# Reordering the first projection, two block seams and the last tiles of a one-core graph network kernel

## Chip, core and metric

The kernel runs on one core of a Trainium2 chip. The metric is the device time of one execution in microseconds (us), the median of several runs. Engines: TensorE (PE; PEld is its weight load), VectorE (DVE), ScalarE (ACT), GpSimd (POOL) and SyncE (SP, which issues the DMAs).

## What is computed

Four graph layers in a row on `x` (2048 × 256) and a 0/1 adjacency (2048 × 2048, mean density about 0.001), each with a residual and a layer norm:

```
x = _layernorm(x + _L0_gnn_ref(x, adj, L0_gnn_W_stack), axis=-1)
x = _layernorm(x + _L1_gnn_ref(x, adj, L1_gnn_W), axis=-1)
x = _layernorm(x + _L2_gnn_ref(x, adj, L2_gnn_W_neigh, L2_gnn_b_neigh, L2_gnn_W_self, L2_gnn_b_self), axis=-1)
x = _layernorm(x + _L3_gnn_ref(x, adj, L3_gnn_W1, L3_gnn_b1, L3_gnn_W2, L3_gnn_b2), axis=-1)
...
# L0, for each of two layers:  proj = x @ W; Wh, Ws = split(proj)
#   a = softmax(Wh @ Ws.T) * adj;  x = leaky_relu(a @ Wh + x)
# L1: relu(A_norm @ H @ W), A_norm = D^-1/2 (A + I) D^-1/2
# L2: relu((adj / deg) @ h @ W_neigh.T + b_neigh + h @ W_self.T + b_self)
# L3: h = relu(adj @ (x @ W1) + b1);  adj @ (h @ W2) + b2
```

## The kernel before

Products keep fp32 accuracy by splitting operands: ScalarE copies a value rounded (the high part, names ending in `_h`), VectorE subtracts it from the original (the low part, `_l`), and TensorE runs high × high, high × low and low × high (`exact3`). Each engine has its own instruction list, written by hand and run in order; semaphores join them. A waiting instruction holds up everything behind it on its engine. `NT` = 16 row tiles of 128 rows, `NCH` = 4 chunks of 512 columns (4 tiles each, `TPC`), `KT` = 2 halves of the 256 features.

**The start.** TensorE runs 8 fill products (`keep_busy`), transposes the first 512 rows of `x` (`features(0)`, one bank for each half of the features), runs 3 more fill products, and then projects queries and keys chunk by chunk. For the first chunk `project_part` makes the two query halves one after the other, six products each into a bank of `scores`, and all of it waits for the low part of the query weights (`s_wgl`). ScalarE makes the high parts of the transposed features, GpSimd the high part of the query weights, VectorE the low parts.

**The blocks.** After two attention layers come the blocks: block 1 (L1), block 2 (L2), block 3a and 3b (the two products with the adjacency of L3). In the code they are `C`, `Dg`, `E` and `F`, and `aggs[k]`. The transposed adjacency lies in `adjr` as the stationary operand; the moving operand is `pm` (512 columns: high and low half), for block 3a `pme` (256 columns). `sum_over(k, t, first, stop)` adds the products of row tile `t` over input tiles `first` to `stop` into one of 4 banks (`sums`: `ob`, a part of `scores`, `tb0`, `tb1`), so tile `t + 4` needs the bank that VectorE's `total` of tile `t` has read. `chunk(k, c, tiles)` is 4 products for each tile named. Tiles 0 to 3 are summed first, as far as their moving operand is ready; `body` sums tiles 4 to 15, 48 chunks, and puts between them the steps of tiles 0 to 13:

- a *turn* (`C_rows`, `D_rows`): TensorE transposes a finished, normalized tile, as soon as VectorE has written its rows (`xs` in block 1, `keep` in block 2);
- a *projection* (`C_project`, `D_project`): the products with the next block's weights, as soon as ScalarE and VectorE have made `xt_h` and `xt_l` of the turned tile.

Tiles 14 and 15 are turned and projected at the *seam*, among the first sums of the next block. VectorE's list for a tile is `total`, `rows_lo` of the tile before, `residual` (add, statistics, variance), `norm` (after ScalarE's root: inverse, normalized rows), `self_term` and `moving_lo`. At the first seam `split(q)` also makes the low part of block 2's moving operand, in five pieces of 4, 4, 4, 2 and 2 tiles, behind ScalarE's high part.

**The end.** `across_sums` sums block 3b for groups of tiles, `sums_hi` and `sums_lo` split a group's sums (at the tiles in `LEAD` = 0, 4, 8, 11, 13), `F_project` makes the last product of each tile, and VectorE adds the residual (`with_residual`), then `statistics`, `mean_variance`, `inverse`, `normed`. SyncE stores each tile.

Of the kernel before, what the change touches and what calls it, by code (L numbers as in the profile page):

```python
# [13 lines left out]
P = 128  # L14
# [29 lines left out]
def ge(eng, signal, count):  # L44

    if isinstance(count, int) and count <= 0:
        return
    if isinstance(signal, Signal):
        eng.wait_ge(signal.sem, count + signal.base)
    else:  # L50
        eng.wait_ge(signal, count)
# [8 lines left out]
def adjacency_resnet(nc, x, adj, w_gat, w_gcn, w_neigh, b_neigh, w_self, b_self, w1, b1, w2, b2, out):  # L60
    N, D = x.shape
    NT = N // P
    KT = D // P
    CH = 512
# [23 lines left out]
    with ctx:  # L88
# [1127 lines left out]
        def _(dve):  # L1216
# [599 lines left out]
            def exact():  # L1816

                for k, a in enumerate(aggs):
                    _, rows_lo, total, residual, norm, self_term, steps = parts(k, a, True)
                    with_residual, statistics, mean_variance, inverse, normed, moving_lo = steps  # L1820
                    split = parts(k + 1, aggs[k + 1], True)[0] if not a.last else None

                    def slot(b, u, ep=True, fin=True):
                        p, pp = before(b, u), before(b, u, 2)
                        if ep:
                            total(*p)
                        if fin:
                            rows_lo(*pp)
                        if ep:
                            residual(*p)  # L1830
                            norm(*p)
                        if fin:
                            self_term(*pp)
                            moving_lo(*pp)

                    if a is F:
                        for t in range(NT + 1):
                            y, z = (t // 2 * 2, t % 2), ((t - 1) // 2 * 2, (t - 1) % 2)
                            if t in LEAD:
                                sums_lo(LEAD.index(t))  # L1840
                            if t < NT:
                                with_residual(*y)
                            if t:
                                inverse(*z)
                            if t < NT:
                                statistics(*y)
                            if t:
                                normed(*z)
                            if t < NT:
                                mean_variance(*y)  # L1850
                        continue
                    if a is E:
                        for t in range(NT):
                            total(t // 2 * 2, t % 2)
                            if t:
                                hidden_lo(t - 1)
                        hidden_lo(NT - 1)
                        continue
                    slot(0, 1, fin=False)
                    slot(2, 0)  # L1860
                    slot(2, 1)
                    unrolled(slot)
                    slot(NT - 2, 0)
                    if not a.last:
                        total(NT - 2, 0)
                        rows_lo(NT - 4, 1)
                        residual(NT - 2, 0)
                        if a is C:
                            split(0)
                        norm(NT - 2, 0)  # L1870
                        self_term(NT - 4, 1)
                        moving_lo(NT - 4, 1)
                        if a is C:
                            split(1)
                        total(NT - 2, 1)
                        rows_lo(NT - 2, 0)
                        residual(NT - 2, 1)
                        norm(NT - 2, 1)
                        if a is C:
                            split(2)  # L1880
                        self_term(NT - 2, 0)
                        moving_lo(NT - 2, 0)
                        if a is C:
                            split(3)
                        rows_lo(NT - 2, 1)
                        self_term(NT - 2, 1)
                        moving_lo(NT - 2, 1)
                        if a is C:
                            split(4)
# [9 lines left out]
        def _(pe):  # L1899
            def mm(o, l, r, start, stop):  # L1900
                return nc.tensor.matmul(o, l, r, start=start, stop=stop)  # L1901
# [34 lines left out]
            def keep_busy(n):  # L1936

                for _ in range(n):
                    mm(xb0[:, 0:P], ident[:, :], ident[:, :], True, True)

            keep_busy(8)
            features(0)
            keep_busy(3)

            def n_rows(t, u):
                pe.wait_ge(n_new, t + 1)
# [12 lines left out]
            def layer(l, g, previous):  # L1959
# [3 lines left out]
                pe.sem_inc(g.wsl.sem, 1)  # L1963
                pe.sem_inc(g.staged.sem, 1)
                pe.sem_inc(g.vl.sem, 1)
                pe.wait_ge(s_wgl[l], 1)
                if l:
                    ge(pe, G[l - 1].ex, 4 * NT)

                def rows_turned(i):  # L1970
# [6 lines left out]
                def project_part(i, o, bank):  # L1977

                    gs, os = bass.ts(i, CH), slice(o * P, (o + 1) * P)
                    if not l and isinstance(i, int) and i + o == 0:  # L1980

                        for k in range(KT):
                            pe.wait_ge(s_x0l, k + 1)
                            mm(bank[:, :], wg_h[:, k, os], xtall_h[:, k, gs], k == 0, False)
                            mm(bank[:, :], wg_h[:, k, os], xtall_l[:, k, gs], False, False)
                            last = mm(bank[:, :], wg_l[:, k, os], xtall_h[:, k, gs], False, k == KT - 1)
                        last.then_inc(g.prod.sem, 1)
                        return
                    exact3(bank[:, :], [(wg_h[:, k, os], wg_l[:, k, os], xtall_h[:, k, gs], xtall_l[:, k, gs])
                                        for k in range(KT)]).then_inc(g.prod.sem, 1)  # L1990

                def project(i):

                    if l or i:
                        rows_turned(i)
                    for o in range(2 * KT):
                        if not l and o == KT:
                            features(i + 1)
                            if i == 0:
                                pe.wait_ge(s_wgl[0], 2)  # L2000
                        if o < KT:
                            ge(pe, g.staged, KT * i + 1)
                        else:
                            ge(pe, g.wsl, KT * i + 1)
                        if l and o == 2 * KT - 1:
                            ge(pe, G[l - 1].z, NT)
                        project_part(i, o, scores[:, o * CH:(o + 1) * CH])
# [298 lines left out]
            def exact():  # L2306
# [45 lines left out]
                def chunk(k, c, *tiles):  # L2352
                    for t in tiles:
                        sum_over(k, t, c * TPC, (c + 1) * TPC)
# [67 lines left out]
                def body(k, rows, project):  # L2422

                    ended = iter([(step, i) for i in range(NT) for step in (rows, project)])

                    def steps(n):
                        for _ in range(n):
                            step, i = next(ended)
                            step(*tile(i))

                    parts, total = NCH * (NT - BANKS), 2 * (NT - 2)
                    for t in range(BANKS, NT):
                        for c in range(NCH):
                            chunk(k, c, t)
                            if project:
                                n = NCH * (t - BANKS) + c
                                steps((n + 1) * total // parts - n * total // parts)

                chunk(0, 0, 0, 1, 2, 3)
# [5 lines left out]
                end_sums(0, NT - NCH)  # L2445
                body(0, C_rows, C_project)

                C_rows(NT - 2, 0)
                chunk(1, 0, 0, 1)
                C_project(NT - 2, 0)  # L2450
                chunk(1, 0, 2, 3)
                chunk(1, 1, 0, 1)
                C_rows(NT - 2, 1)
                chunk(1, 1, 2, 3)
# [2 lines left out]
                end_sums(1, NT - NCH)  # L2457
                body(1, D_rows, D_project)

                D_rows(NT - 2, 0)  # L2460
                chunk(2, 0, 0, 1)
                D_project(NT - 2, 0)
                chunk(2, 0, 2, 3)
                chunk(2, 1, 0, 1, 2, 3)
                chunk(2, 2, 0, 1)
                D_rows(NT - 2, 1)
                chunk(2, 2, 2, 3)
                for t in range(BANKS):
                    sum_over(2, t, NT - 4, NT - 2)
                D_project(NT - 2, 1)  # L2470
                for t in range(BANKS):
                    sum_over(2, t, NT - 2, NT - 1)
                end_sums(2, NT - 1)
                body(2, None, None)

                across_sums(0, 0, NT)
# [40 lines left out]
```

## Time and profile before

| | |
|---|---|
| three runs | 735.72, 736.05 (median), 737.24 us |
| profiled execution | 736.77 us; span from first to last instruction 735.0 us |
| TensorE busy | 719.0 us (98%), 3984 products |
| VectorE, ScalarE, GpSimd busy | 481.4, 337.3, 324.6 us |
| mean granted TensorE clock | 0.997 |

A busy share is a mean over stages. Matmuls are pipelined, so one of 512 columns is shown with about 0.4 us though the next starts 0.23 us after it: spacing is read from start to start. In a row of the timeline the bracket at the end is the idle time of that engine before the row, and what ended it.

### The profile page before, as it was taken

The page shows a single profiled execution, that of the slowest core. Times are in us where ns is not written, and L with a number is a line of the kernel's source. Part 1 is how long each engine was busy: PE and PEld are TensorE (multiplying, and loading weights), DVE is VectorE, ACT ScalarE, POOL GpSimd, SP SyncE. Part 2 cuts the span into 40 slices and gives each one's busy share as a digit, 9 for nine tenths or more (in the row PEclk, how much of TensorE's full clock was granted, in tenths as well). Part 3 has the DMA queues.
Part 4 walks back from the last instruction along what each step waited for, and adds up shares of the span by engine and source line. Part 5 has one row for each costly group of instructions (what it writes and reads, how often), then busy time and mean ns, then how long its engine had stood idle before and what let it go on. Part 6 is the DMA issues. An engine that isn't in the chain of part 4 may idle for free.

```text
span 735.0 us, 13241 instructions
## 1 busy us (share of the span) xinstructions
PE 719.0 (98%) x3984; PEld 613.1 (83%) x3984; DVE 481.4 (66%) x1111; ACT 337.3 (46%) x785; POOL 324.6 (44%) x346
## 2 busy tenths in 40 slices
PE   8999999999999999999999999999999999989995
PEld 7888888888888888888888888888777687779985
DVE  3767777777776664655755755754677848875366
ACT  4666565665656455365465465451222412221121
POOL 1157676676766316454454454384664000003200
PEclk9999999999999999999999999999999999999998
DMA  7042424324242201732231232246862222210012
GB/s 271 29 144 93 166 87 144 113 101 156 86 153 76 111 18 58 166 119 74 87 128 71 86 128 72 86 103 126 194 171 87 72 64 66 66 44 2 1 44 74
DMA packets 63139, 72.39 MB, mean 98 GB/s; under 512 B 36336, under 2 KB 56432, under 8 KB 58992
## 3 DMA queue, kind: packets, MB, share of 16 engines
q1 hardware_dynamic: 63088, 71.78, 31.3%
q8 instruction: 24, 0.39, 0.2%
q14 instruction: 27, 0.22, 0.1%
HBM read 46.60 MB, written 16.78 MB: 86 GB/s over the span
## 4 chain that ended last, share of the span: by engine, by line
PE 93%; DVE 3%; issue 1%; ACT 1%; POOL 1%; DMA 0%; SPq 0%; DVEq 0%; POOLq 0%; ACTq 0%
PE scores L1901 39%; PE ob L1901 29%; PE tb L1901 11%; PE tb L2070 7%; PE xb L1901 3%; PE tb L2014 1%; DMA self_term_scratch<-rst 0%; PE tb L1920 0%; PE xb L2095 0%; PE xb L1949 0%; POOL adjr L648 0%; SPq L477 0%; DVE xt_l L1222 0%; PE scores L2371 0%; DVE zb L1611 0%
## 5 line engine op out<-in xcount | busy, mean ns | idle before, releaser
L671 POOL TENSOR_TENSOR prob<-prob,arow 128x512 f32<-128x512 f32 x128 | 191.9, 1521 | 145.9 <-ACT prob L875 145.8
L1901 PE MATMUL ob<-val,stationary 128*128 128x512 f32 x960 | 186.7, 344 | 0.0
L1901 PEld LDWEIGHTS ob<-val,stationary 128*128 128x128 f32 x960 | 146.7, 189 | 18.4
L1222 DVE TENSOR_TENSOR stationary<-tb,stationary 128x512 fp32r<-128x512 f32 x128 | 85.4, 687 | 57.3 <-ACT stationary L776 56.1
L1901 PE MATMUL scores<-wst_h,whs_h 128*128 128x512 f32 x256 | 102.6, 401 | 0.0
L1901 PE MATMUL scores<-wst_h,whs_l 128*128 128x512 f32 x256 | 100.0, 390 | 0.0
L1901 PE MATMUL scores<-wst_l,whs_h 128*128 128x512 f32 x256 | 99.8, 390 | 0.0
L1319 DVE TENSOR_REDUCE row_values<-scores 128x1 f32<-128x512 f32 x128 | 85.9, 683 | 13.5 <-PE scores L1901 12.0
L776 ACT ACTIVATE stationary<-tb 128x512 fp32r<-128x512 f32 x128 | 72.9, 595 | 42.4 <-PE tb L2070 40.9
L875 ACT ACTIVATE prob<-scores,row_values 128x512 f32<-128x512 f32 x128 | 86.8, 690 | 11.4 <-DVE row_values L1326 11.4
L2070 PE MATMUL tb<-ident,prob 128*128 128x128 f32 x512 | 71.7, 272 | 0.0
L1901 PE MATMUL tb<-pm,adjr 128*128 128x512 f32 x256 | 66.7, 399 | 0.0
L2070 PEld LDWEIGHTS tb<-ident,prob 128*128 128x128 f32 x512 | 60.0, 140 | 5.7
L733 POOL TENSOR_TENSOR keep<-keep,bout 128x256 f32 x16 | 11.7, 743 | 106.7 <-PE tb L1901 101.1
L1061 ACT ACTIVATE sd<-mv,constants 128x1 f32<-128x1 f32 x48 | 14.1, 295 | 93.6 <-DVE mv L1691 93.6
L1901 PEld LDWEIGHTS scores<-wst_h,whs_l 128*128 128x128 f32 x256 | 48.1, 188 | 10.3
L1901 PEld LDWEIGHTS scores<-wst_h,whs_h 128*128 128x128 f32 x256 | 48.1, 188 | 9.3
L1901 PEld LDWEIGHTS scores<-wst_l,whs_h 128*128 128x128 f32 x256 | 48.3, 189 | 7.9
L1901 PEld LDWEIGHTS tb<-pm,adjr 128*128 128x128 f32 x256 | 46.3, 188 | 9.0
L1359 DVE SCALAR_TENSOR_TENSOR arow<-arow 128x2048 bf16<-128x2048 f32 x16 | 43.6, 2725 | 3.0 <-issue 3.0
L776 ACT ACTIVATE xt_h<-xb 128x256 fp32r<-128x256 f32 x30 | 11.5, 384 | 62.4 <-PE xb L1949 43.7
L648 POOL CAST adjr<-at 128x512 fp32r<-128x512 bf16 x64 | 40.0, 668 | 0.0
(227 smaller groups left out, 1191.7 us busy)
## 6 DMA issues: line engine op xcount, KB each, us to landing
arow<-in_adj SPq DMA_DIRECT2D x32, 1024.0 KB, 5.2
adjacency_halves<-arow SPq DMA_DIRECT2D x16, 512.0 KB, 3.0
features_scratch<-xs SPq DMA_DIRECT2D x32, 128.0 KB, 1.9
xres<-features_scratch SPq DMA_DIRECT2D x32, 128.0 KB, 2.1
keep<-in_x SPq DMA_DIRECT2D x4, 512.0 KB, 7.2
xres<-in_x SPq DMA_DIRECT2D x16, 128.0 KB, 2.0
self_term_scratch<-rst SPq DMA_DIRECT2D x16, 128.0 KB, 1.7
rin<-self_term_scratch SPq DMA_DIRECT2D x16, 128.0 KB, 2.2
```

The lines of the kernel that those rows point to most:

```text
L648: nc.gpsimd.tensor_copy(adjr[:, t, js.start * P:js.stop * P], at16[r][:, js, :].rearrange("p a i -> p (a i)")).then_inc(s_conv, 1)
L671: nc.gpsimd.tensor_tensor(prob[u][:, cs], prob[u][:, cs], arow[u][:, cs], ALU.mult).then_inc(g.msk.sem, 1)
L733: nc.gpsimd.tensor_tensor(keep[:, t, :], keep[:, t, :], bout[:, :], ALU.add).then_inc(s_kb, 1)
L776: return nc.scalar.activation(dst, src, ACT.Copy, **kw)
L875: nc.scalar.activation(prob[u][:, cs], scores[:, cs], ACT.Exp, bias=nmax[u][:, :], accum_out=rs[u][:, c:c + 1]).then_inc(g.ex.sem, 1)
L1061: nc.scalar.activation(sd[:, u:u + 1], mv[:, u, 1:2], ACT.Sqrt, bias=eps[:, :])\
L1222: return nc.vector.tensor_tensor(dst, v, h.bitcast(F32), ALU.subtract)
L1319: nc.vector.reduce_max(mx[u][:, c:c + 1], scores[:, c * CH:(c + 1) * CH], AX.X)\
L1359: nc.vector.scalar_tensor_tensor(arow16[:, :], arow[u][:, :], 1.0, arow16[:, :], ALU.mult, ALU.not_equal, accum_out=bits[:, bass.ds(t, 1)])\
L1901: return nc.tensor.matmul(o, l, r, start=start, stop=stop)
L2014: last = nc.tensor.transpose(bank[:, at:at + P], wht_g[:, k, (2 * h + a) * P:(2 * h + a + 1) * P], ident[:, :])
L2070: last = nc.tensor.transpose(tb[c % 2][:, q * P:(q + 1) * P], prob[u][:, j * P:(j + 1) * P], ident[:, :])
```

## The change

At the start the three fill products are taken out, and the first chunk's query halves are made side by side by `first_queries`: the high × high products as soon as their operands are there, then the others, each pair with a wait of its own. In `body` the steps are spread over 47 chunks and not 48, so the last projection stands ahead of the last chunk. At both seams sums of the next block stand ahead of the turn of tile 14, and VectorE's order at the first seam follows: the first piece of `split` ahead of tile 14's `residual`, the second behind tile 15's `total`. In block 3b `sums_lo` of the groups at tiles 11 and 13 stands behind that tile's add and statistics, and the last tiles' steps are interleaved.

```diff
                     if a is F:
-                        for t in range(NT + 1):
+                        for t in range(NT - 2):
                             y, z = (t // 2 * 2, t % 2), ((t - 1) // 2 * 2, (t - 1) % 2)
-                            if t in LEAD:
+                            if t in LEAD and t <= TPC * 2:
                                 sums_lo(LEAD.index(t))
...
                             if t:
                                 inverse(*z)
-                            if t < NT:
-                                statistics(*y)
+                            statistics(*y)
+                            if t in LEAD and t > TPC * 2:
+                                sums_lo(LEAD.index(t))
                             if t:
                                 normed(*z)
...
+                        inverse(NT - 4, 1)
+                        normed(NT - 4, 1)
+                        with_residual(NT - 2, 0)
+                        statistics(NT - 2, 0)
+                        with_residual(NT - 2, 1)
+                        mean_variance(NT - 2, 0)
+                        statistics(NT - 2, 1)
+                        inverse(NT - 2, 0)
+                        mean_variance(NT - 2, 1)
+                        normed(NT - 2, 0)
+                        inverse(NT - 2, 1)
+                        normed(NT - 2, 1)
...
                         total(NT - 2, 0)
                         rows_lo(NT - 4, 1)
-                        residual(NT - 2, 0)
                         if a is C:
                             split(0)
+                        residual(NT - 2, 0)
                         norm(NT - 2, 0)
                         self_term(NT - 4, 1)
                         moving_lo(NT - 4, 1)
+                        total(NT - 2, 1)
+                        rows_lo(NT - 2, 0)
                         if a is C:
                             split(1)
-                        total(NT - 2, 1)
-                        rows_lo(NT - 2, 0)
                         residual(NT - 2, 1)
...
             features(0)
-            keep_busy(3)
...
+                def first_queries():
+
+                    def both(w, x, k, start=False):
+                        return [mm(scores[:, o * CH:(o + 1) * CH], w[:, k, o * P:(o + 1) * P], x[:, k, 0:CH],
+                                   start, False) for o in range(KT)]
+
+                    pe.wait_ge(s_wqh, 1)
+                    for k in range(KT):
+                        pe.wait_ge(s_x0h, k + 1)
+                        both(wg_h, xtall_h, k, k == 0)
+                    pe.wait_ge(s_x0l, 1)
+                    both(wg_h, xtall_l, 0)
+                    pe.wait_ge(s_wgl[0], 1)
+                    for k in range(KT):
+                        both(wg_l, xtall_h, k)
+                    pe.wait_ge(s_x0l, KT)
+                    for o in range(KT):
+                        mm(scores[:, o * CH:(o + 1) * CH], wg_h[:, 1, o * P:(o + 1) * P], xtall_l[:, 1, 0:CH],
+                           False, True).then_inc(g.prod.sem, 1)
...
-                    parts, total = NCH * (NT - BANKS), 2 * (NT - 2)
+                    parts, total = NCH * (NT - BANKS) - 1, 2 * (NT - 2)
...
-                            if project:
-                                n = NCH * (t - BANKS) + c
+                            n = NCH * (t - BANKS) + c
+                            if project and n < parts:
                                 steps((n + 1) * total // parts - n * total // parts)
...
+                chunk(1, 0, 0, 1)
                 C_rows(NT - 2, 0)
-                chunk(1, 0, 0, 1)
+                chunk(1, 0, 2, 3)
                 C_project(NT - 2, 0)
-                chunk(1, 0, 2, 3)
                 chunk(1, 1, 0, 1)
...
+                chunk(2, 0, 0, 1)
+                chunk(2, 1, 0, 1)
                 D_rows(NT - 2, 0)
-                chunk(2, 0, 0, 1)
+                chunk(2, 2, 0, 1)
+                chunk(2, 0, 2)
                 D_project(NT - 2, 0)
-                chunk(2, 0, 2, 3)
-                chunk(2, 1, 0, 1, 2, 3)
-                chunk(2, 2, 0, 1)
+                chunk(2, 0, 3)
+                chunk(2, 1, 2, 3)
                 D_rows(NT - 2, 1)
                 chunk(2, 2, 2, 3)
-                for t in range(BANKS):
+                for t in range(2):
                     sum_over(2, t, NT - 4, NT - 2)
                 D_project(NT - 2, 1)
-                for t in range(BANKS):
-                    sum_over(2, t, NT - 2, NT - 1)
-                end_sums(2, NT - 1)
+                for t in range(2, BANKS):
+                    sum_over(2, t, NT - 4, NT - 1)
+                for t in range(2):
+                    sum_over(2, t, NT - 2, NT)
+                for t in range(2, BANKS):
+                    sum_over(2, t, NT - 1, NT)
```

TensorE's list at the first seam, before, from the last chunk of block 1 to the first sums of block 2 (`scores<-w2h,xt_h` begins a projection of six products, `xb<-ident,xs` is the turn of tile 14):

```order
L1901 MATMUL tb<-pm,adjr 128x512 x4
L1901 MATMUL scores<-w2h,xt_h 128x512 [waits agg_self_term_ready,agg_projection_kept,agg_rows_lo]
...
L2236 MATMUL xb<-ident,xs 128x128 [waits agg_rows_lo,agg_rows_ready]
...
L1901 MATMUL ob<-pm,adjr 128x512 [waits agg_moving_lo_block2,agg_sum_ready]
...
L1901 MATMUL scores<-pm,adjr 128x512 [waits agg_moving_lo_block2,agg_sum_ready]
```

The same place after:

```order
L1912 MATMUL scores<-w2h,xt_h 128x512 [waits agg_self_term_ready,agg_projection_kept,agg_rows_lo]
...
L1912 MATMUL tb<-pm,adjr 128x512 x4
L1912 MATMUL ob<-pm,adjr 128x512 [waits agg_moving_lo_block2,agg_sum_ready]
...
L1912 MATMUL scores<-pm,adjr 128x512 [waits agg_moving_lo_block2,agg_sum_ready]
...
L2261 MATMUL xb<-ident,xs 128x128 [waits agg_rows_lo,agg_rows_ready]
```

The projection of tile 13 went ahead of the last chunk, and the first two chunks of block 2 went ahead of the turn of tile 14.

TensorE's list at the second seam, before, from the last chunk of block 2 to the projection of tile 14 (`pme` products are block 3a's, `xb<-ident,keep` is the turn of tile 14):

```order
1523 L1901 MATMUL tb<-pm,adjr 128x512 x4
1524 L1901 MATMUL scores<-w3a,xt_h 128x256
...
1528 L2371 MATMUL xb<-ident,keep 128x128 x2
1529 L1901 MATMUL ob<-pme,adjr 128x256 x4
1530 L1901 MATMUL scores<-pme,adjr 128x256 x4
1531 L1901 MATMUL scores<-w3a,xt_h 128x256
```

The same place after:

```order
1520 L1912 MATMUL tb<-pm,adjr 128x512 x4
1521 L1912 MATMUL ob<-pme,adjr 128x256 x4
1522 L1912 MATMUL scores<-pme,adjr 128x256 x4
1523 L1912 MATMUL ob<-pme,adjr 128x256 x4
1524 L1912 MATMUL scores<-pme,adjr 128x256 x4
1525 L2396 MATMUL xb<-ident,keep 128x128 x2
1526 L1912 MATMUL ob<-pme,adjr 128x256 x4
1527 L1912 MATMUL scores<-pme,adjr 128x256 x4
1528 L1912 MATMUL tb<-pme,adjr 128x256 x4
1529 L1912 MATMUL scores<-w3a,xt_h 128x256
```

Sixteen products of block 3a now stand ahead of the turn of tile 14, and twelve between the turn and the projection where there were eight.

VectorE's list at the end, before, tiles 14 and 15 behind the normalization of tile 12 (the add reads `scores` and `keep`, `xs` and `xres` take the normalized rows):

```order
1259 L1691 BN_AGGR mv<-norm_values 128x2
1260 L1661 TENSOR_TENSOR zb<-scores,keep 128x256
1261 L1701 RECIPROCAL rstd<-sd 128x1
1262 L1684 BN_STATS norm_values<-zb 128x6
1263 L1720 TENSOR_SCALAR xres<-zb,mv,rstd 128x256
1264 L1691 BN_AGGR mv<-norm_values 128x2
1265 L1701 RECIPROCAL rstd<-sd 128x1
1266 L1720 TENSOR_SCALAR xres<-zb,mv,rstd 128x256
```

The same place after:

```order
1255 L1701 RECIPROCAL rstd<-sd 128x1
1256 L1720 TENSOR_SCALAR xs<-zb,mv,rstd 128x256
1257 L1661 TENSOR_TENSOR zb<-scores,keep 128x256
1258 L1684 BN_STATS norm_values<-zb 128x6
1259 L1661 TENSOR_TENSOR zb<-scores,keep 128x256
1260 L1691 BN_AGGR mv<-norm_values 128x2
1261 L1684 BN_STATS norm_values<-zb 128x6
1262 L1701 RECIPROCAL rstd<-sd 128x1
1263 L1691 BN_AGGR mv<-norm_values 128x2
1264 L1720 TENSOR_SCALAR xres<-zb,mv,rstd 128x256
1265 L1701 RECIPROCAL rstd<-sd 128x1
1266 L1720 TENSOR_SCALAR xres<-zb,mv,rstd 128x256
```

Tile 13 is now finished before tile 14 begins, and the adds and statistics of tiles 14 and 15 stand ahead of the inverses of both.

## Rows read from the trace of the kernel before

**Rows 1.** The page: its head, busy time of the engines, and the chain that ended last.

```profile
span 735.0 us, 13241 instructions
...
PE 719.0 (98%) x3984; PEld 613.1 (83%) x3984; DVE 481.4 (66%) x1111; ACT 337.3 (46%) x785; POOL 324.6 (44%) x346
...
PE 93%; DVE 3%; issue 1%; ACT 1%; POOL 1%; DMA 0%; SPq 0%; DVEq 0%; POOLq 0%; ACTq 0%
```

**Rows 2.** Timeline of the start: start, length, engine, line, operation, count, idle before.

```profile
5.12 1.91 PE L1920 MATMUL tb<-ident,keep 128*128 128x128 f32 x8
...
6.82 0.96 PE L1901 MATMUL xb<-ident 128*128 128x128 f32 x6
...
7.07 0.60 ACT L776 ACTIVATE xtall_h<-tb 128x512 fp32r<-128x512 f32 x1 [0.26 <-PE tb L1920]
...
8.19 0.49 PE L1901 MATMUL scores<-xtall_h,wg_h 128*128 128x512 f32 x1 [0.41 <-DVE wg_l L1222]
```

**Rows 3.** Chain that ended last, at the start: start, length, engine, output, count.

```profile
8.19 3.06 PE scores L1901 x12
11.25 0.88 PE tb L1920 x8
12.12 2.77 PE scores L1901 x12
```

**Rows 4.** Timeline of TensorE, block 1's last tiles and the first seam.

```profile
567.07 0.38 PE L2236 MATMUL scores<-ident,xs 128*128 128x128 f32 x2
...
580.87 0.44 PE L2236 MATMUL xb<-ident,xs 128*128 128x128 f32 x2 [1.13 <-DVE xs L1727]
...
583.58 0.51 PE L1901 MATMUL scores<-w2h,xt_h 128*128 128x512 f32 x1 [0.41 <-DVE xt_l L1222]
```

**Rows 5.** Timeline of VectorE, block 1's last tiles and the first seam.

```profile
565.86 0.41 DVE L1727 TENSOR_SCALAR xs<-zb,mv,rstd 128x256 f32<-128x256 f32 x1
...
579.10 1.19 DVE L1222 TENSOR_TENSOR pm<-keep,pm 128x1024 fp32r<-128x1024 f32 x1
...
580.41 0.41 DVE L1727 TENSOR_SCALAR xs<-zb,mv,rstd 128x256 f32<-128x256 f32 x1
```

**Rows 6.** Timeline of TensorE, the second seam.

```profile
656.68 0.44 PE L2371 MATMUL xb<-ident,keep 128*128 128x128 f32 x2 [1.46 <-DVE keep L1709]
...
658.45 0.39 PE L1901 MATMUL scores<-w3a,xt_h 128*128 128x256 f32 x1 [0.38 <-DVE xt_l L1222]
...
662.84 0.38 PE L2371 MATMUL scores<-ident,keep 128*128 128x128 f32 x2
...
664.96 0.28 PE L1901 MATMUL scores<-w3a,xt_h 128*128 128x256 f32 x1
...
667.73 2.19 PE L1901 MATMUL ob<-pme,adjr 128*128 128x256 f32 x16 [0.36 <-DVE zb L1608]
```

**Rows 7.** Timeline of VectorE in block 2, normalized rows of tiles 4, 14 and 15.

```profile
616.51 0.41 DVE L1709 TENSOR_SCALAR keep<-zb,mv,rstd 128x256 f32<-128x256 f32 x1
...
656.21 0.41 DVE L1709 TENSOR_SCALAR keep<-zb,mv,rstd 128x256 f32<-128x256 f32 x1
...
660.12 0.41 DVE L1709 TENSOR_SCALAR keep<-zb,mv,rstd 128x256 f32<-128x256 f32 x1
```

**Rows 8.** Timeline of VectorE in block 3b, its first tile and its last.

```profile
701.08 0.43 DVE L1684 BATCH_NORM_STATS2 norm_values<-zb 128x6 f32<-128x256 f32 x1
701.66 0.18 DVE L1691 BATCH_NORM_AGGREGATE mv<-norm_values 128x2 f32<-128x6 f32 x1 [0.16 <-DVE norm_values L1684]
...
726.30 0.42 DVE L1222 TENSOR_TENSOR fsum_l<-xb,fsum_h 128x256 fp32r<-128x256 f32 x1 [0.79 <-ACT fsum_h L776]
726.64 0.41 DVE L1661 TENSOR_TENSOR zb<-scores,keep 128x256 f32<-128x256 f32 x1
...
730.95 0.16 DVE L1701 RECIPROCAL rstd<-sd 128x1 f32<-128x1 f32 x1 [0.36 <-ACT sd L1061]
731.14 0.41 DVE L1720 TENSOR_SCALAR xres<-zb,mv,rstd 128x256 f32<-128x256 f32 x1
```

More of the change, by code:

```diff
@@ L1836, in exact @@
                     if a is F:
-                        for t in range(NT + 1):
+                        for t in range(NT - 2):
                             y, z = (t // 2 * 2, t % 2), ((t - 1) // 2 * 2, (t - 1) % 2)
-                            if t in LEAD:
+                            if t in LEAD and t <= TPC * 2:
                                 sums_lo(LEAD.index(t))
-                            if t < NT:
-                                with_residual(*y)
+                            with_residual(*y)
                             if t:
                                 inverse(*z)
-                            if t < NT:
-                                statistics(*y)
+                            statistics(*y)
+                            if t in LEAD and t > TPC * 2:
+                                sums_lo(LEAD.index(t))
                             if t:
                                 normed(*z)
-                            if t < NT:
-                                mean_variance(*y)
+                            mean_variance(*y)
+                        inverse(NT - 4, 1)
[10 more added lines that the diff above has]
+                        normed(NT - 2, 1)
                         continue
@@ L1965, in layer @@
                 pe.sem_inc(g.vl.sem, 1)
-                pe.wait_ge(s_wgl[l], 1)
                 if l:
+                    pe.wait_ge(s_wgl[l], 1)
                     ge(pe, G[l - 1].ex, 4 * NT)
@@ L1979, in project_part @@
                     gs, os = bass.ts(i, CH), slice(o * P, (o + 1) * P)
[L1980 to L1988, printed above, removed]
                     exact3(bank[:, :], [(wg_h[:, k, os], wg_l[:, k, os], xtall_h[:, k, gs], xtall_l[:, k, gs])
                                         for k in range(KT)]).then_inc(g.prod.sem, 1)
+                def first_queries():
[15 more added lines that the diff above has]
+                           False, True).then_inc(g.prod.sem, 1)
                 def project(i):
@@ L1995, in project @@
                         rows_turned(i)
+                    else:
+                        first_queries()
                     for o in range(2 * KT):
+                        if not l and isinstance(i, int) and i == 0 and o < KT:
+                            continue
                         if not l and o == KT:
```

## The prediction

> **What bounds the kernel.** I read the page first, then TensorE's waits, then the rows around each place that the diff touches. The page gives TensorE 719.0 of 735.0 us [rows 1]: at most 16.0 us of the span are without a matmul, so an edit can win only by closing a named hole, or by shortening the stretch after the last matmul. In the chain that ended last 93% is TensorE [rows 1]; between the start and the first seam its matmuls follow each other at 0.23 us for 512 columns (twelve in 2.77 us [rows 3]). What is won at the start is therefore handed on: nothing later waits for a clock time, only for TensorE's own products.
>
> The holes that the diff touches are these. At the start the first product waits until 8.19 us for VectorE's low part of the query weights, 0.41 us of it idle [rows 2]; three fill products stand before it. At the first seam TensorE waits 1.13 us for the new rows of tile 14, and 0.41 us for their low part [rows 4]. At the second seam the same two waits are 1.46 and 0.38 us, and one of 0.36 us ends the seam [rows 6]. Behind the last matmul VectorE finishes three tiles one after the other, and the last has to wait 0.36 us for its root [rows 8].
>
> **The start.** Before, twelve products run from 8.19 to 11.25 us: 12 × 0.23 and 0.29 for starting up [rows 3]. After, the first two need only the first copy of the high features and the high query weights, and run where the fill stood (6.82 [rows 2]). The next two need the second high copy, which ends at 7.07 + 0.60 = 7.67 [rows 2]. I allow 0.06 for the release: ten products from 7.73 on end at 7.73 + 2.30 + 0.29 = 10.32. The low weights come before the seventh product (7.73 + 0.29 + 4 × 0.23 = 8.94, against 8.19), so that wait is covered. Gain 11.25 − 10.32 = 0.93 us. The query banks are now released together, not one after the other, but ScalarE copies the next features first and comes to them later anyway. Bounds: 0.5 (a second start-up and a late copy) and 0.95. I take 0.9.
>
> The three fill products are taken out, so what do they do for TensorE's clock? The granted clock reads full in the page, but the rows show two speeds: the first eight transposes take 1.91 us [rows 2], eight equal ones at 11.25 take 0.88 [rows 3], as 1.2 against 2.4 GHz would give. The six fill records take 0.96 us together, the quicker pace already [rows 2]. So the rise came before or while the first of them ran, after eight plain products and the transposes, and they cannot have caused it. By the Trainium skill ("TensorE: Matmul & The Clock Gate", Part 4: PE-mode transpose) transposes do not count as activity for the clock; by that rule removing plain products just here would be the wrong edit, and the time that of rival (c) below, 735.1. This trace leaves it open, since eight plain products stood ahead of the transposes, but the fill was not needed here.
>
> **The first seam (block 1 to block 2).** Before, TensorE is ready for the turn of tile 14 at 580.87 − 1.13 = 579.74, and VectorE ends the rows at 580.41 + 0.41 = 580.82 [rows 4, 5]. After, eight sum products (8 × 0.23 = 1.85) stand ahead of that turn, so TensorE comes at 581.6, some 0.8 after the rows. VectorE's low half of block 2's first moving piece (1.19 us [rows 5]) is put ahead of tile 14's residual; it was already inside that chain, between variance and root, where 0.36 of it lay beside ScalarE. So it costs the rows between 0 and 0.4 us, inside the 0.8. The 0.41 us: before the low part of tile 14 stood behind the second such piece and tile 15's total; now the piece stands behind it, and eight products lie between turn and projection as before. The sums moved up need the first piece (long ready by then) and, for the fourth bank, tile 15's total, which is now ahead of the second piece. So both waits go: 1.54 us, and two restarts at 0.1 to 0.29 [rows 3].
>
> Against it: the bodies now spread 28 turns and projections over 47 chunks, not 48, so in the second half most turns come one chunk (4 × 0.23 = 0.92) sooner. In block 1 tile 11's rows end at 565.86 + 0.41 = 566.27 and its turn is at 567.07 [rows 5, 4]: 0.80 spare, 0.12 too little. Such a shortage is paid once, since a late TensorE is late for the next turn too; I put 0.3 to 0.5 us for the whole body. Net 1.54 + 0.3 − 0.4 = 1.4 us; bounds 0.8 and 1.9.
>
> **The second seam (block 2 to block 3).** Here VectorE sets the pace: from 616.51 to 656.21 it ends ten tiles, 3.97 us each [rows 7], while TensorE's share of a tile is 48 × 0.92 / 14 = 3.2 and some 0.5 for a turn and a projection, 3.7. A turn one chunk sooner only waits there, at no cost to VectorE. Before, TensorE is ready for turn 14 at 656.68 − 1.46 = 655.22. After, sixteen products of 256 columns (2.19 with a restart [rows 6], so 0.12 apart) stand ahead of it: 657.2, or 658.0 if TensorE first lost 0.9 in the body. The rows are there at 656.21 + 0.41 = 656.62 [rows 7]: no wait. The price is that tile 14's turn, and with it VectorE's next step, comes 0.5 to 1.3 later, so tile 15's rows slip from 660.53 to about 661.3. They had room: TensorE turned them only at 662.84, 2.31 after they were done [rows 6, 7]. After, 24 half-width products and a projection lie between the turns (24 × 0.12 + 0.5 = 3.4), so turn 15 is at 661.4. From there to the last projection there were sixteen products (662.84 to 664.96, 2.12), now twelve (1.6), hence 663.0; the path through the low part to the first tile of block 3 (664.96 to 667.73, 2.77) is unchanged. 665.8 against 667.73: 1.9. I take 1.8; bounds 0.9 and 2.2. All is counted from the start of block 2, which the first seam moves.
>
> **The end.** VectorE's steps start 0.31 to 0.34 apart where none waits [rows 8]. Before, from the last low half (726.30) to the end of the last normalization (731.14 + 0.41) are 5.25 us. After, tile 13's add and statistics stand ahead of that low half, in time in which VectorE waited for ScalarE. Behind it come, start to start: low half 0.34, normalization of 12 0.31, variance of 13 to its inverse 0.54 (0.18 and the 0.36 wait), inverse 0.19, normalization 0.31, add of 14 0.43, statistics 0.34, add of 15 0.34, variance of 14 0.21, statistics of 15 to variance 0.58 (701.08 to 701.66), variance to inverse 0.54, inverse 0.19, normalization 0.41: 4.73. Gain 0.5 us; bounds 0.2 (the last two stores now lie about half a microsecond apart) and 0.6. The other low half, at tile 11, is some 0.4 us later; TensorE's product that needs it has about 0.1 to spare.
>
> **Sum.** 0.9 + 1.4 + 1.8 + 0.5 = 4.6 us. The profiled execution took 736.77 (span 735.0 and 1.77 around it), 0.72 above the median of the runs shown, 736.05. So 732.2 for that execution, 730.4 in span, and 731.5 for the median.
>
> **Rivals.** (a) *The waits only move on.* At both seams half of the gain is taken by the next in-order step of VectorE (the second piece behind tile 14's low part; tile 15's rows at the second seam): 0.9 + 0.7 + 0.9 + 0.4 = 2.9, 733.1. For it: every cover is a margin of under 1 us. (b) *The seams give nothing*, since VectorE's chain and not TensorE's order sets the end of each block: 0.9 + 0.5 = 1.4, 734.7. Against it: at the second seam tile 15's rows lie 2.31 us idle. (c) *The clock stays low at the start* without the fill: twelve products and eight transposes at double time cost 2.77 + 0.88 = 3.65; the seams remain: 736.05 − 4.6 + 3.65 = 735.1, no difference. (d) *Slower: the turns come too soon.* If VectorE is the pace in block 1 as in block 2, TensorE waits up to a chunk at each of the six turns shifted, 5.6 us there, and with the same again in block 2 11.1, against the 4.6 gained: 742.6. It decides from 6.1 us of new waits in the bodies on. Against it: the 0.80 spare at tile 11, and that such waits do not add up.
>
> **How the numbers follow.** Forecast 0.66 (730.2 to 732.6), (a) 0.17, (b) 0.08, (c) 0.05, (d) 0.04. The range 730.2 to 733.9 takes in the forecast and (a) with its bounds. Faster by over 0.2% (1.47 us, about what a measurement of this kernel tells from no change) means below 734.6: forecast and (a), and a little of (b): 0.85. Same: most of (b), and (c): 0.11. Slower: (d): 0.04.
>
> **What would show it.** In the changed profile: the first product at about 6.9 and the first values' transposes 0.9 us sooner; no wait of TensorE for tile 14's rows or low part at either seam; in block 2 waits for rows spread over the body; half a microsecond less between TensorE's last product and the last normalization. The forecast is wrong if transposes at 10 us still take 0.2 us each, if a new wait of about a microsecond stands in a seam, or if block 1's body shows more than half a microsecond of new waits.

## The result, and the profile after

The changed kernel takes 731.08 us (median of four runs, 730.37 to 732.37); the kernel before, beside it, 736.64. The ratio is 0.9926 with a 95% interval of 0.9904 to 0.9948: 3.8 to 7.1 us less, about 5.5. A second group of runs on another chip gave 730.88 against 735.74, 0.9938 (0.9921 to 0.9955). The forecast was 731.5 us, 4.6 less. The profiled execution took 732.37 us with a span of 730.6.

The page of the changed kernel, as [rows 1]: its head, busy times, and the chain that ended last.

```profile
span 730.6 us, 13229 instructions
PE 718.5 (98%) x3978; PEld 611.8 (84%) x3978; DVE 482.6 (66%) x1111; ACT 337.1 (46%) x785; POOL 324.7 (44%) x346
PE 93%; DVE 2%; ACT 1%; issue 1%; SPq 1%; DMA 1%; POOL 1%; DVEq 0%; POOLq 0%; ACTq 0%
```

TensorE's busy time hardly moved; its holes did: the span without a matmul is 12.1 us, before 16.0. The timeline of TensorE at the start, as [rows 2, 3]:

```profile
5.12 1.92 PE L1931 MATMUL tb<-ident,keep 128*128 128x128 f32 x8
6.96 1.49 PE L1912 MATMUL scores<-xtall_h,wg_h 128*128 128x512 f32 x4
9.65 0.62 PE L1912 MATMUL scores<-xtall_l,wg_h 128*128 128x512 f32 x2
10.11 1.03 PE L1931 MATMUL tb<-ident,keep 128*128 128x128 f32 x8
```

The first product is at 6.96, and the first values' transposes at 10.11, where the timeline of before has them at 11.08. They are at the quick pace without the fill. The first seam, TensorE and then VectorE, as [rows 4, 5]:

```profile
580.88 0.38 PE L2261 MATMUL xb<-ident,xs 128*128 128x128 f32 x2
582.96 0.39 PE L1912 MATMUL scores<-w2h,xt_h 128*128 128x512 f32 x1
586.20 0.38 PE L2261 MATMUL scores<-ident,xs 128*128 128x128 f32 x2
```
```profile
579.42 0.41 DVE L1727 TENSOR_SCALAR xs<-zb,mv,rstd 128x256 f32<-128x256 f32 x1
581.72 0.42 DVE L1222 TENSOR_TENSOR xt_l<-xb,xt_h 128x256 fp32r<-128x256 f32 x1 [0.64 <-ACT xt_h L776]
```

Neither row of TensorE for tile 14 (580.88 turn, 582.96 projection) has a bracket: both waits of [rows 4] are gone. The rows of tile 14 end at 579.83, 1.05 ahead of the turn, their low part at 582.14, 0.82 ahead of the projection. The second seam, as [rows 6]:

```profile
655.12 0.38 PE L2396 MATMUL xb<-ident,keep 128*128 128x128 f32 x2
656.77 0.28 PE L1912 MATMUL scores<-w3a,xt_h 128*128 128x256 f32 x1
658.66 0.38 PE L2396 MATMUL scores<-ident,keep 128*128 128x128 f32 x2
663.07 2.18 PE L1912 MATMUL ob<-pme,adjr 128*128 128x256 f32 x16 [0.24 <-DVE zb L1608]
```

Turn 14 (655.12) and its projection (656.77) wait for nothing; the wait that ends the seam is 0.24 us, before 0.36. VectorE's last low half and last normalization, as [rows 8]:

```profile
721.60 0.43 DVE L1222 TENSOR_TENSOR fsum_l<-xb,fsum_h 128x256 fp32r<-128x256 f32 x1
722.80 0.16 DVE L1701 RECIPROCAL rstd<-sd 128x1 f32<-128x1 f32 x1 [0.36 <-ACT sd L1061]
725.91 0.41 DVE L1720 TENSOR_SCALAR xres<-zb,mv,rstd 128x256 f32<-128x256 f32 x1
```

From the one to the other are 4.31 us, before 4.84. But the span ends 4.69 us after 725.91, and before 3.86 after 731.14. What the end won came back behind it, in this profile.

### The profile page after: what moved, and what is told of

Same layout as the page of the kernel before. It is cut to its first block, busy times and chain, and to the rows that moved or that the text cites. A ratio compares the mean times of both kernels' runs of the same rounds, so it can differ in the third digit from the quotient of the medians.

```text
span 730.6 us, 13229 instructions
## 1 busy us (share of the span) xinstructions
PE 718.5 (98%) x3978; PEld 611.8 (84%) x3978; DVE 482.6 (66%) x1111; ACT 337.1 (46%) x785; POOL 324.7 (44%) x346
## 4 chain that ended last, share of the span: by engine, by line
PE 93%; DVE 2%; ACT 1%; issue 1%; SPq 1%; DMA 1%; POOL 1%; DVEq 0%; POOLq 0%; ACTq 0%
PE scores L1912 39%; PE ob L1912 29%; PE tb L1912 11%; PE tb L2095 7%; PE xb L1912 3%; PE tb L2039 1%; SPq L477 1%; PE tb L1931 1%; DMA self_term_scratch<-rst 0%; PE xb L2120 0%; PE xb L1959 0%; POOL adjr L648 0%; DMA xres<-features_scratch 0%; PE scores L2396 0%; PE xb L2396 0%
```

## The experiments

All twelve kernels were profiled and timed, in three groups of four on one chip each. The first four each do one part of the change on the kernel before, with that part of the diff shown above; the bodies stay spread over 48 chunks in them.

**The start alone.** The edit: `first_queries`, no three fill products.

> The kernel before with the new start alone (first queries side by side, high products first, no three fill products). My theory: 0.9 to 1.0 us less, so 735.1 where the kernel before takes 736.05; the first values' transposes at about 10.1 us and still some 0.9 us for eight. Rival, the clock stays low without the fill: those transposes take 1.9 us and the time is no lower or up to 2.7 us higher. Rival, the lead is lost again at the seams, where VectorE's chain sets the pace: no change, and longer waits in the seams by as much.

Measured: 0.9986 (0.9976 to 0.9996), 1.0 us less; first values' transposes at 10.12. At both seams the waits stand as long as before (1.13 and 0.41 us, 1.47 and 0.38), 0.8 to 0.9 us sooner: nearly the whole lead is handed on.

**The first seam alone.** The edit: TensorE's order at the seam, VectorE's order of the two pieces.

> The kernel before with the first seam alone (eight sum products ahead of tile 14's turn, VectorE's two pieces moved), bodies spread over 48 chunks as before. My theory: both waits of TensorE for tile 14 at that seam (1.13 and 0.41 us) and two restarts go, 1.5 to 1.9 us less. Rival, the waits only move on: 0.7 us less and a new wait of TensorE at that seam. Rival, VectorE's chain sets the block's end: no change, the wait stands at tile 15 or in block 2's body.

Measured: 0.9973 (0.9963 to 0.9983), 2.0 us less. The turns of tiles 13 and 15 are 10.11 us apart (576.38 to 586.49), before 11.97 (576.77 to 588.74): 1.86, the two waits and the restarts, with no new wait.

**The second seam alone.** The edit: TensorE's order at that seam.

> The kernel before with the second seam alone, bodies spread over 48 chunks as before. My theory: the waits of 1.46 and 0.38 us at that seam go, the one that ends it stays, 1.8 to 2.1 us less. Rival, the waits only move on (tile 15's rows come late): 0.9 us less, TensorE waiting about 1 us at tile 15's turn. Rival, VectorE's chain sets the end: no change.

Measured: 0.9962 (0.9948 to 0.9976), 2.8 us less, more than expected. Turns 14 and 15 and the last wait of the seam:

```profile
657.31 0.38 PE L2371 MATMUL xb<-ident,keep 128*128 128x128 f32 x2
660.87 0.44 PE L2371 MATMUL scores<-ident,keep 128*128 128x128 f32 x2
665.34 0.85 PE L1901 MATMUL ob<-pme,adjr 128*128 128x256 f32 x5 [0.23 <-DVE zb L1608]
```

From block 2's first turn (601.57) to 665.34 are 63.77 us, before 66.41 (601.32 to 667.73): 2.64. It is more than the two waits of 1.46 and 0.38 us and the restarts behind them, since the two waits in front of the last products shrink as well, from 0.58 and 0.36 us (at 666.63 and 667.73 before) to 0.22 and 0.23 (at 664.25 and 665.34). What the time shows beyond 2.64, 0.2 us, lies far inside its interval (1.8 to 3.8 us less).

**The end alone.** The edit: VectorE's last tiles interleaved.

> The kernel before with VectorE's last tiles interleaved and nothing else. My theory: the last normalization ends 0.5 us sooner after TensorE's last product, and the time falls by 0.5 us. Rival, the stores take it back: in the profile of the changed kernel the last store is issued 0.64 us after the one ahead of it, not 1.05, and lands after 3.7 us, not 2.9; by this the last normalization ends 0.5 us sooner and the time does not change or rises by up to 0.3 us.

Measured: 0.9996 (0.9987 to 1.0005), no change that can be told; the interval goes from 1.0 us less to 0.4 more, so it does not rule out the expected 0.5 by itself. The rows speak for the rival. The last normalization is 4.33 us behind the last low half, but the span ends 3.99 us after it. The last stores of its profile:

```profile
L593 SPq DMA_DIRECT2D out_rows<-xres x2: 332/332/333, 731.8 to 732.4; - x2
DMA to landing us min/median/max: 3.0/3.2/3.3
```

They are issued 0.6 us apart and land 3.3 and 3.0 us after their issue; two of the same profile, at 725.1 and 726.5, took 1.7 each.

**The fill put back, and no fill at all.** Both are edits of the changed kernel:

```diff
 keep_busy(8)
 features(0)
+keep_busy(3)
```
```diff
-keep_busy(8)
 features(0)
```

> The changed kernel with the three fill products put back behind the first transposes. My theory: they are not needed for the clock; the first two products, which could run at 6.96 us, come behind 0.96 us of fill (six records), the next two wait for the second high copy anyway (7.72), so the start loses 0.3 to 0.5 us and no more. Rival, the fill holds the clock up: the first four products get quicker and the time falls by 0.2 us or more.

> The changed kernel without the eight plain products ahead of the first transposes, so that TensorE has done nothing but transposes before its first products. My theory, transposes raise the clock as products do: the transposes of 10 us take some 0.9 us for eight and the time is within 0.5 us of the changed kernel's. Rival, the rule that transposes do not count: the twelve first products take twice as long (0.23 us more each, 2.8 us in all) and the transposes behind them 1.9 us; the time rises by 1.5 to 3.7 us.

Measured with the fill back: 0.9937 (0.9923 to 0.9951), the changed kernel's own ratio, and no gain. The loss of 0.3 to 0.5 us that I expected is too small for this interval; in its profile there is none. The first product stands at 6.81 behind the fill, and at 6.82 without it in the profile of the second run of the changed kernel, whose clock also rose early (rows in the last section): there TensorE waits 0.34 us for ScalarE's copy, and the fill lies largely in that time. No profile has the fill with a clock that rises late, as in the changed kernel's first profile. Without any: 0.9950 (0.9935 to 0.9964), 1.0 us slower than the kernel with the fill beside it, and by the ratios 0.9 to 1.8 slower than the changed kernel in its two groups. TensorE's start there:

```profile
4.62 1.94 PE L1931 MATMUL tb<-ident,keep 128*128 128x128 f32 x8 [4.62 <-DMA keep<-in_x]
6.51 2.07 PE L1912 MATMUL scores<-xtall_h,wg_h 128*128 128x512 f32 x4
8.38 1.05 PE L1912 MATMUL scores<-xtall_l,wg_h 128*128 128x512 f32 x2
9.23 1.21 PE L1912 MATMUL scores<-xtall_h,wg_l 128*128 128x512 f32 x4
10.73 1.03 PE L1931 MATMUL tb<-ident,keep 128*128 128x128 f32 x8
```

The first six products start 0.42 to 0.47 us apart, half speed, the last six 0.23 to 0.26; the values' transposes are at 10.73. My limit of half a microsecond was too small, and the rival, all twelve at half speed and the transposes too, is wrong as well.

**VectorE's order at the first seam as before.** The edit, in the changed kernel (each `if` joined with its body on one line):

```diff
 rows_lo(NT - 4, 1)
-if a is C: split(0)
 residual(NT - 2, 0)
+if a is C: split(0)
 ...
+if a is C: split(1)
 total(NT - 2, 1)
 rows_lo(NT - 2, 0)
-if a is C: split(1)
```

> The changed kernel with VectorE's own order at the first seam as before (first piece between tile 14's variance and root, second piece and tile 15's total ahead of tile 14's low part). My theory, from the changed kernel's rows: the low part then ends near 582.5 us, still ahead of tile 14's projection at 582.96, so no change, at most 0.2 us. Rival, VectorE's order is what took the 0.41 us wait away: 0.4 to 0.8 us more, with TensorE waiting for that low part.

Measured: 0.9933 (0.9919 to 0.9947), no difference. TensorE's turn of tile 14 is at 579.84, its projection at 581.91, neither with a wait; VectorE's rows and low part are there in time:

```profile
577.88 0.41 DVE L1727 TENSOR_SCALAR xs<-zb,mv,rstd 128x256 f32<-128x256 f32 x1
578.54 1.22 DVE L1222 TENSOR_TENSOR pm<-keep,pm 128x1024 fp32r<-128x1024 f32 x1
580.67 0.42 DVE L1222 TENSOR_TENSOR xt_l<-xb,xt_h 128x256 fp32r<-128x256 f32 x1
```

The second piece fills the time in which VectorE waits for ScalarE's half (0.64 us at that place in the changed kernel). With the old order the rows of tile 14 even end 1.55 us ahead of the turn (578.29 and 579.84), with the new one 1.05: a piece moved ahead of them only used up cover. At this seam TensorE's order did all of the work, with the bodies over 47 chunks; over 48, where the cover of the rows is 0.14 us in the next experiment's profile (579.79 and 579.93), VectorE's old order was not run.

**The bodies spread over 48 chunks.** The edit, in the changed kernel:

```diff
-parts, total = NCH * (NT - BANKS) - 1, 2 * (NT - 2)
+parts, total = NCH * (NT - BANKS), 2 * (NT - 2)
```

> The changed kernel with the bodies' turns and projections spread over 48 chunks again, so that those of the second half come one chunk (0.92 us) later. My theory: in block 1 no wait is there to be saved, so 0 to 0.3 us less there; in block 2 the last projection comes closer to the seam, whose rows for tile 14 then are late by up to 0.5 us. Net within 0.5 us of the changed kernel. Rival, the earlier turns cost the bodies 0.4 us or more: faster by that much.

Measured: 0.9914 (0.9900 to 0.9929), 730.12 us; the two kernels beside it, whose edits of the changed one had no measured effect, took 731.55 (fill) and 730.96 (VectorE's order), 0.8 to 1.4 more. The intervals overlap, but the rows bear it out, and with them the rival. From block 2's first turn to the last wait of its seam:

```profile
597.94 0.38 PE L2396 MATMUL xb<-ident,keep 128*128 128x128 f32 x2
661.69 0.50 PE L1912 MATMUL ob<-pme,adjr 128*128 128x256 f32 x2 [0.23 <-DVE zb L1608]
```

63.75 us, and 64.30 in the changed kernel (598.77 to 663.07). No wait of TensorE's for tile 14's rows came, as I had thought it might. Where the 0.55 us go can be read from the starts of TensorE's products between block 2's first turn and its turn 14. Mostly they start 0.23 us apart, at some places up to 0.32; at nine turns and projections it is 0.38 to 0.45 in each of the six profiles with 47 chunks, at six in each of the eight with 48. Three more pauses of some 0.17 us make 0.5.

**The changed kernel once more, and with the old end.** The second takes back the interleaved end.

> The changed kernel once more, beside the three others of this group on one chip. My theory, from the rows of the runs so far: 4.5 to 5.5 us less than the kernel before. It is the measure for the other three and for the fill and body experiments, whose differences from the changed kernel are under 1 us.

> The changed kernel with VectorE's order of the last block as before. My theory: the last normalization ends 5.25 us after the start of the last low half, not 4.72, so it ends 0.5 us later; the time rises by 0.2 to 0.5 us. Rival, the stores take back what the interleaving wins, since the last two are issued closer together: the time does not change.

Measured: 0.9938 and 0.9930 (0.9915 to 0.9946): 730.88 and 730.73 us, no difference, the rival again: the old end, which I expected to be 0.2 to 0.5 us slower, is 0.15 quicker in the median. With the old end the last normalization is 4.85 us behind the low half, but the span ends 3.62 us after it.

**A version with both bodies at 48, and the end further interleaved.** The edit of the end:

```diff
+with_residual(NT - 2, 0)
 inverse(NT - 4, 1)
 normed(NT - 4, 1)
-with_residual(NT - 2, 0)
```

> The changed kernel with the bodies spread over 48 chunks and, at the end, tile 14's add ahead of tile 13's inverse, where VectorE waits 0.36 us for a root. My theory: from the first turn of block 2 to the last wait of its seam 63.75 us, not 64.30 (so in the run with 48 alone), and 0.4 us less in block 1; at the end 0.3 us less from the last low half to the last normalization: 0.8 to 1.3 us less than the changed kernel. Rival, the end's part is lost behind the last normalization, in the stores: 0.5 to 0.9 us less, and the last store lands later after its issue.

Measured: 0.9924 (0.9908 to 0.9940), 730.20 us, 0.7 under the changed kernel beside it, with intervals that overlap. Block 2 takes 63.76 us as at 48; the last normalization is 3.95 us behind the low half, and the span ends 4.85 after it. So by these rows the gain is the bodies', and the end's is lost in the stores. No version here was better than the spread over 48.

**The wait of the second seam filled.** The kernel before, with plain products in that wait (the loop on one line):

```diff
 body(1, D_rows, D_project)
+ge(pe, Dg.xtl, NT - 3)
+for _ in range(8): mm(xb[0][:, 0:P], ident[:, :], ident[:, :], True, True)
 D_rows(NT - 2, 0)
```

> The kernel before with eight plain products (sixteen records, about 1.1 us) put into TensorE's wait for tile 14's rows at the second seam. The wait itself stays. Theory, the wait lets TensorE's clock fall in some executions: the granted clock is 1.00 in the microseconds behind that seam in the profile, no execution has a mean clock of 0.994 or less, and the median falls by 0 to 0.3 us. Rival, the falls come from elsewhere: one execution in six still shows them.

Measured: 1.0001 (0.9990 to 1.0012); no time is won. The products take 1.84 us (654.51 to 656.35), not the 1.1 that I reckoned, so they take the whole wait, and turn 14 comes 0.2 us later after block 2's first turn than before (55.59 and 55.36). None of its twelve executions has a mean granted clock under 0.996. What the clock has to do with it can be seen in a profile in which the wait is not filled: the kernel with the end alone, at the second seam, which its edit does not touch (windows of 4 us: TensorE's busy time, granted clock, DMA):

```profile
654.00:658.00 4.00, 2.48 (x16) 1.00 0.00 0
658.00:662.00 4.00, 3.66 (x18) 0.57 0.02 4
662.00:666.00 4.00, 4.00 (x36) 1.00 0.00 0
```
```profile
656.57 0.44 PE L2382 MATMUL xb<-ident,keep 128*128 128x128 f32 x2 [1.46 <-DVE keep L1709]
659.25 2.02 PE L1912 MATMUL tb<-pme,adjr 128*128 128x256 f32 x8
664.26 0.38 PE L2382 MATMUL scores<-ident,keep 128*128 128x128 f32 x2
```

The same eight products of 256 columns in the profile of the filled kernel:

```profile
658.42 1.17 PE L1901 MATMUL tb<-pme,adjr 128*128 128x256 f32 x8
```

Behind the waits of 1.46 and 0.38 us the clock falls to its lower level (0.51 from 658.3 to 661, so 1.2 of 2.4 GHz), the eight products take 2.02 us and not 1.17, and turn 15 comes 7.69 us after turn 14, not 6.16 as in [rows 6]. That costs 1.5 us.

## Why the forecast was right, and where its terms were off

The intervals below are start to start, from the timelines of the fourteen profiles; "n" is how many profiles each mean has. Where the bodies were at 48 or 47 makes a difference, and is named.

| interval | before's order | changed, 48 | changed, 47 | gain by rows | forecast |
|---|---|---|---|---|---|
| start to first values' transposes | 11.08 (n 5) | 9.85 (n 7, either) | | 1.2 | 0.9 |
| from there to turn 15 of block 1 | 577.60 (n 5) | 575.33 (n 3) | 575.73 (n 6) | 1.9 | 1.4 |
| block 2's first turn to the seam's last wait | 66.44 (n 3; two with a fallen clock 67.95) | 63.76 (n 3) | 64.30 (n 6) | 2.1 | 1.8 |
| last low half to last normalization | 4.85 (n 6) | 4.32 (n 7, either) | | 0.5 | 0.5 |
| last normalization to end of span | 3.59 (n 6) | 4.26 (n 7, either) | | −0.7 | 0 |

The start is without the two fill experiments, the last two rows without the further interleaved end. The rows add up to 5.1, but 0.4 of the second row is scatter and not the change's (below). A fall of the clock that costs 1.5 us in about one execution of six adds some 0.25, so about 4.9. The runs say 4.6 and 5.5. The forecast's 4.6 lies with them partly by luck: three terms were too small, and the one of the end too large.

*The start* was right as a mechanism. Its size was for the clock as [rows 2] have it, with eight slow transposes; in other executions the clock rises earlier and the values' transposes come sooner, by 0.7 us at the most (9.39 against 10.13). Before, the wait for the low weights hid this. Rival (c) falls: fill or not, the transposes behind the first products are quick.

*The first seam*: both waits gone without a successor, 1.86 us against the 1.84 put down for them. The body's price, put at 0.3 to 0.5, is 0.4. The other 0.4 of that row lie ahead of turn 13 of block 1: from the values' transposes to there before's order takes 565.6 us in the mean, and 565.2 with the bodies at 48, though TensorE's and VectorE's lists are the same in that stretch. Before's order differs by 0.9 there among its own five profiles, and the largest part of that is one wait of TensorE for a tile's low part, 0.50 us with the second seam alone (at 529.93), 0.28 in the kernel before (at 529.72), and none with the filled wait. The step that gave VectorE's moved pieces a share in the 0.41 us was wrong: TensorE's order alone took that wait away.

*The second seam*: the order is worth 2.7 (66.44 less 63.76), and the forecast reckoned 0.8 off for a body that lags (turn 14 at 658.0, not 657.2); the measured lag is 0.54. So the term comes to 2.1, not 1.9. The sentence that a turn one chunk sooner only waits there was half right: the pauses are there, as the forecast's signs have them, three of some 0.17 us, but each is paid at the end, since TensorE waits for nothing at the changed seam until its last products.

*The end* is the term that failed. The working up to the last normalization came out (0.53), and the bound named the last two stores, half a microsecond apart; but the sum took 0.5, and by the rows nothing is left of it: 4.85 and 3.59 us before are 8.44, 4.32 and 4.26 after are 8.58. The times of the two experiments show no gain either, though the first alone could not rule out 0.5. The last store lands later after its issue by 0.7, at 3.3 us in the mean of the seven profiles with the new end (2.5 to 3.7), 2.6 in the six with the old (2.2 to 2.9). Rival (a), half of each gain taken by the next in-order step, and (b) fall with the seams; (d) falls since block 1's body shows no long wait and both bodies together cost under 1 us.

## What to carry to other kernels

Read the gain of a reordering to the end of the span, not to the last instruction of an engine: here the last store landed later by at least as much as it was issued sooner. Where an edit has several parts, run each alone: here one part of TensorE's order brought the most, VectorE's brought nothing, the new spread of the bodies cost 0.9 us, and the whole hid all three. A wait of TensorE can cost about its own length a second time when the clock falls behind it (1.5 us behind one of 1.46), in some executions only, which one profile need not show.

## What the runs showed of the hardware

**The clock can fall behind a wait of 1.46 us.** Of the executions of kernels that have that wait, 16 of 92 show a mean granted clock of 0.994 or less (in the first group the medians of before's are 737.5 us for these and 736.2 for the rest); of kernels whose second seam has no such wait, 0 of 52; with the wait filled, 0 of 12. Two executions without the wait stand at 0.995, next to that line. Two profiles show the fall itself, both right behind the waits of this seam (the end alone and the first seam alone); two others with the same waits show none, and of the other executions only the mean clock is known. So that the wait brings the fall rests on these counts; that filling cures it is likely but not certain, since at 16 in 92 twelve executions would show none one time in ten.

**The clock's rise at the start moves.** After the same eight plain products the eight transposes at 5.12 took 1.92, 1.61, 1.36 and 1.26 us in four executions. This is the changed kernel, run a second time:

```profile
5.12 1.36 PE L1931 MATMUL tb<-ident,keep 128*128 128x128 f32 x8
6.82 1.17 PE L1912 MATMUL scores<-xtall_h,wg_h 128*128 128x512 f32 x4 [0.34 <-ACT xtall_h L776]
9.68 1.03 PE L1931 MATMUL tb<-ident,keep 128*128 128x128 f32 x8
```

The Trainium skill ("TensorE: Matmul & The Clock Gate", Part 1: What's actually happening) says that the chip's window of activity runs free of the kernel's start, so that the moment of the rise varies with where the first matmul falls in it. The traces agree in that the moment varies; the window itself no run shows. Whether transposes count for the clock (the Trainium skill, same page, Part 4: PE-mode transpose, says they do not) stays open: with transposes alone ahead, the first six products ran at half speed, which fits the rule, but in no run do transposes alone stand ahead of a rise.

**The last stores land late.** Stores of the last block issued earlier mostly land after 1.7 us; the last ones take up to 4.0 (in the changed kernel the two last, at 725.7 and 726.4, took 4.0 and 3.7; in before's, at 730.5 and 731.6, 3.6 and 2.9). The distance to the store ahead is not all of it: in before's profile the one at 727.9 took 2.5 us, 2.4 behind the one ahead, and the one at 725.5, 1.4 behind, 1.7. Nor is it the last two alone: in the changed kernel those at 722.4 and 723.4 took 3.3 and 2.6, and in five profiles the last but one landed after 1.7. What they wait for was not tried, and stays open.
